# A graph layer on one NeuronCore: the maximum with zero of the messages moved from ScalarE to VectorE, and more rows fetched outside GpSimd

## The reference

```python
ef  = relu(edge_attr @ We1 + be1) @ We2 + be2        # 64 -> 128 -> 128
tw  = sigmoid(edge_weight[:, None] @ Wt + bt)
ef  = ef * tw
msg = relu(concatenate([x[src], ef], 1) @ Wn1 + bn1) @ Wn2 + bn2
out = segment_sum(msg, dst, num_segments=6250) + x
y   = layernorm(x + out)
```

## Time and profile before

| | |
|---|---|
| median of 3 runs | 1044.24 us (1042.26 to 1045.14) |
| the profiled execution | 1044.55 us |
| its span, first to last instruction | 1043.1 us |
| mean granted clock of TensorE | 0.956 of full speed |
| PE busy | 851.1 us (82%) |
| POOL busy | 776.5 us (74%) |
| DVE busy | 648.9 us (62%) |
| ACT busy | 494.9 us (47%) |

### The profile page before, as it was taken

One profiled execution on the slowest core, in us unless ns is written; L12 is line 12 of the kernel. 1 busy time (PEld: TensorE's weight loads), 2 busy tenths in 40 slices (PEclk: granted clock), 3 DMA queues, 4 the chain that ended last, 5 costly groups with the idle time before them and its releaser, 6 DMA issues.

```text
span 1043.1 us, 22424 instructions
## 1 busy us (share of the span) xinstructions
PE 851.1 (82%) x5035; PEld 616.5 (59%) x5036; DVE 648.9 (62%) x1682; ACT 494.9 (47%) x674; POOL 776.5 (74%) x825
## 2 busy tenths in 40 slices
PE   6989996988888778778787778878877877888884
PEld 6766665665556565555565555555555555565653
DVE  4767774775756665755557566566566566557566
ACT  5565454455445345444345445445444444444443
POOL 7777777777777777777777777777777777777772
PEclk9999999999999999999999999999999999999997
DMA  8984555555555554554545555455455455455311
GB/s 231 278 239 124 146 146 146 140 150 140 135 156 142 144 155 118 145 154 133 137 138 137 137 143 155 117 146 154 115 147 146 126 146 143 127 149 142 83 53 48
DMA packets 159417, 148.90 MB, mean 143 GB/s; under 512 B 123479, under 2 KB 127894, under 8 KB 159270
## 3 DMA queue, kind: packets, MB, share of 16 engines
q1 hardware_dynamic: 129062, 89.99, 31.0%
q0 software_dynamic: 26080, 53.46, 20.0%
q10 hardware_dynamic: 4128, 3.87, 1.2%
HBM read 140.85 MB, written 6.40 MB: 141 GB/s over the span
## 4 chain that ended last, share of the span: by engine, by line
POOL 44%; issue 22%; PE 12%; DMA 7%; DVE 6%; SPq 3%; ACT 3%; ACTq 1%; DVEq 1%; POOLq 0%
POOL gathered L566 44%; DMA gathered<-node_table,src_e 5%; PE psS L896 4%; PE psM L938 3%; PE psE L963 2%; DVE h L1220 2%; PE psH L951 2%; SPq L537 2%; DMA x_sb<-in_x 1%; DVE onehot L1226 1%; ACT h L656 1%; DMA ew<-in_edge_weight 1%; ACT tw L724 1%; ACTq L652 1%; DVE efw L1241 1%
## 5 line engine op out<-in xcount | busy, mean ns | idle before, releaser
L566 POOL DMA_INDIRECT gathered<-node_table,src_e x767 | 729.3, 951 | 234.0 <-issue 228.2
L729 ACT ACTIVATE h<-psH,be_c 128x1024 f32<-128x1024 f32 x104 | 115.9, 1114 | 443.1 <-PE psH L951 435.1
L896 PE MATMUL psS<-onehot,h 128*128 128x128 f32 x1656 | 226.4, 292 | 67.6 <-ACT h L656 65.7
L896 PEld LDWEIGHTS psS<-onehot,h 128*128 128x128 f32 x1656 | 209.1, 204 | 86.1 <-issue 49.4
L1220 DVE TENSOR_TENSOR h<-psM,gathered 128x1024 f32<-128x1024 f32 (+1 forms) x102 | 120.2, 1180 | 220.8 <-DMA gathered<-node_table,src_e 173.4
L963 PE MATMUL psE<-h,we 128*128 128x512 f32 x416 | 218.3, 649 | 0.0
L938 PE MATMUL psM<-wn,efw 128*128 128x128 f32 x1664 | 208.6, 280 | 4.8 <-DVE h L1220 4.8
L938 PEld LDWEIGHTS psM<-wn,efw 128*128 128x128 f32 x1664 | 200.7, 197 | 5.6 <-DVE h L1220 5.6
L1241 DVE SCALAR_TENSOR_TENSOR efw<-psE,be_c,tw 128x1024 f32<-128x1024 f32 x104 | 133.3, 1281 | 105.6 <-PE psE L963 95.5
L951 PE MATMUL psH<-eaT,we 64*128 64x512 f32 x416 | 120.1, 654 | 66.7 <-DMA gathered<-node_table,src_e 63.3
L1226 DVE TENSOR_SCALAR onehot<-split_ids,dst_e 128x65 f32<-128x65 f32 x832 | 173.9, 272 | 0.0
(11 more groups left out here) (128 smaller groups left out, 363.5 us busy)
## 6 DMA issues: line engine op xcount, KB each, us to landing
ew<-in_edge_weight SPq DMA_DIRECT2D x104, 512.0 KB
ea<-in_edge_attr SPq DMA_DIRECT2D x104, 256.0 KB
fetched<-node_table SPq DMA_DIRECT2D x1408, 0.5 KB
dst_rows<-node_table ACTq DMA_DIRECT2D x768, 0.5 KB
gathered<-node_table,src_e POOLq DMA_INDIRECT x767, 2.5
x_sb<-in_x SPq DMA_DIRECT2D x6, 512.0 KB, 9.0
out_y<-x_sb ACTq DMA_DIRECT2D x12, 256.0 KB
node_table<-gathered SPq DMA_DIRECT2D x7, 256.0 KB, 5.7
```

The lines of the kernel that those rows point to most:

```text
L566: pool.indirect_dma_start(to, None, rows, bass.IndirectOffsetOnAxis(index, 0)).then_inc(landed, by)
L729: nc.scalar.activation(h1[:, s % 2, :], psH[:, :, :].rearrange("p r e -> p (r e)"), ACT.Relu, bias=be1_c[:, :]).then_inc(h1_ready, 1)
L896: return nc.tensor.matmul(to, h[:, (k - SUM_LAG) % BODY * PAIR + q, t * C:(t + 1) * C], hot, start=(t == 0), stop=(t == TILES - 1))
```

## The change

- `FETCHED` starts a pair earlier and runs to pair 102: 12 pairs (14, 22, ..., 102) in place of 11. SP's loop gets two more rounds of `fetch_rows` at its end for it.
- `ACT_FETCHED` follows a list of parts: a first tile at 8 rows a step over 16 steps, then seven at 12 rows a step over 11 steps: 8 pairs (23, 33, 44, 55, 66, 77, 88, 99) in place of 6.
- `CLOSE_FROM` goes from 20 to 40.
- The relu of `h` goes from ACT. DVE makes the maximum with zero in place instead, by one `tensor_scalar` directly behind `pre`, after a wait for it. The last pair keeps its relu on ACT, and so does the first layer.
- In ACT's step the wait for `psS` stays where it was and the copy moves behind the block's copy.
- PE waits in `sums_step` for `sums_ready`, too: the relu that it waited for stood behind that copy on ACT.

```diff
-CLOSE_FROM = 20
+CLOSE_FROM = 40
...
-FETCHED = list(range(15, 96, FETCH_STEPS))
-ACT_ROWS, ACT_STEPS, ACT_FROM = 8, 16, 6
-ACT_FETCHED = list(range(ACT_FROM + ACT_STEPS, 103, ACT_STEPS))
+FETCHED = list(range(14, 103, FETCH_STEPS))
+ACT_FROM, ACT_PARTS = 6, [(8, 16)] + 7 * [(12, 11)]
+ACT_BEGIN = [ACT_FROM + sum(n for _, n in ACT_PARTS[:f]) for f in range(len(ACT_PARTS))]
+ACT_FETCHED = [at + n for at, (_, n) in zip(ACT_BEGIN, ACT_PARTS)]
+ACT_FETCHED = [p + (p in FETCHED) for p in ACT_FETCHED]
...
+            for n in range(PAIRS, FETCHED[-1] + 4):
+                fetch_rows(n)
...
-                f, at = divmod(s - ACT_FROM, ACT_STEPS)
-                if not 0 <= f < len(ACT_FETCHED) or at * ACT_ROWS >= P:
+                f = sum(s >= begin for begin in ACT_BEGIN) - 1
+                if f < 0:
+                    return
+                at, each = s - ACT_BEGIN[f], ACT_PARTS[f][0]
+                if at * each >= P:
                     return
...
                 if live(i, k, ADD_LAG):
-                    copy_sums(s - ADD_LAG, k - ADD_LAG)
+                    act.wait_ge(sum_ps, s - ADD_LAG + 1)
                 if TILE < k <= TILE + BT // 2 and 1 <= i < TURNS:
                     finish_one(act, blocks, low["now"], lambda b: copy_tiles((k - TILE - 1) * 2), False)
-                if live(i, k, H_LAG):
-                    g = s - H_LAG
-                    at = g % BODY * PAIR
-                    act.wait_ge(pre_ready, g + 1)
-                    relu(h[:, at:at + PAIR, :].rearrange("p q e -> p (q e)")).then_inc(h_ready, 1)
+                if live(i, k, ADD_LAG):
+                    copy_sums(s - ADD_LAG, k - ADD_LAG)
...
                     pe.wait_ge(h_ready, s - SUM_LAG + 1)
+                    if not (isinstance(i, int) and s == SUM_LAG):
+                        pe.wait_ge(sums_ready, s - SUM_LAG)
...
                 make_pre(h[:, at, :], psM[:, :, :], rows).then_inc(pre_ready, 1)
+                dve.wait_ge(pre_ready, g + 1)
+                to = h[:, at, :].rearrange("p q e -> p (q e)")
+                nc.vector.tensor_scalar(to, to, 0.0, None, ALU.max).then_inc(h_ready, 1)
```

More of the change, by code:

```diff
@@ L648, in fetch_rows @@
                     act.wait_ge(act_placed, f - 1)
-                parts = range(at * ACT_ROWS, min((at + 1) * ACT_ROWS, P))
+                parts = range(at * each, min((at + 1) * each, P))
                 rows = numbers_of(ACT_ENGINE, ACT_FETCHED[f], parts)
```

## The result

The changed kernel takes 1053.65 us (median of 5 runs, 1052.93 to 1058.01) against 1044.24 us: a ratio of 1.0108, 95% interval 1.0084 to 1.0132. It is slower, by 9.4 us, where 11.1 were forecast. The profiled execution took 1052.93 us, the shortest of the five, its span 1051.1 us.

The account below looks back on a forecast made before the run. GpSimd's stream of gathers was taken as the bound. 1044.55 - 3.8 (fewer gathers) + 14.2 (delayed gathers) + 0.7 (end) = 1055.65, less 0.3 for the median: 1055.3 us, range 1045 to 1062.

Parts of the forecast that it names:

- The bound: GpSimd's stream of 815 gathers, one each 1.256 us with no hole, sets the end; every other engine waits for it.
- Fetched rows: Row copies on SyncE and ScalarE for more pairs: three gathers go, -3.8 us; ScalarE's longer issues cost nothing.
- The third rival: ScalarE becomes the bound, its 12 issues slowing its step past GpSimd's 10 us: 1063 us and up; chance 0.02.
- The limit, ScalarE's order, TensorE's new wait: Running ahead limited from pair 40 for 20, sums copied later, TensorE waiting for copy and maximum: no effect on time.
- The maximum's time: Each of 103 maxima on VectorE, 128x1024 from SBUF to SBUF, takes 0.72 us, bounds 0.67 and 0.77.
- The delay of the gathers: Maxima on VectorE hold up gathers on GpSimd: 47 of 103 hit, 14.2 us in all.
- at one moment: A gather needs something of VectorE's only once, about 0.05 to 0.12 us after its start.
- The fourth rival: A gather has a second such moment, 0.74 to 0.94 us after its start: 1069 us; chance 0.04.
- the rule for the start: A gather's delay is the VectorE instruction's end minus the gather's start minus 0.12 us.
- The weighing of the Trainium skill's rule: VectorE and GpSimd's shared port: rows contradict VectorE being blocked when second; by the rule 11 us instead of 14.2.
- The end: The last maximum, of pair 102, ahead of VectorE's work on the last pair: 0.7 us, bounds 0 and 0.7.
- The first rival: The maximum holds up no gather, only the three fewer gathers count: 1040.5 us, 0.36% faster; chance 0.12.

Follow-up runs that it names:

- the kernels with short gathers and nothing late: Changed kernel with the relu back on ScalarE, 1040.12 us; changed kernel with the sum in PSUM and the maximum from PSUM to SBUF, 1041.20 us.
- the kernel at 1040.12 us: Changed kernel with the relu of the messages back on ScalarE, behind the copy of sums: 1040.12 us, ratio to before 0.9958.

## Why the prediction was right, and where it was not

**The bound** was read rightly: all differences sit in GpSimd's stream and behind it, and the kernels with short gathers and nothing late (1040.12 and 1041.20 us) differ from before by the number of gathers and by what lies behind the last one.

**Fetched rows**: -3.8 us forecast, -4.0 measured with the relu on ScalarE. Nothing for the longer list of issues was right at 12 rows, but the cover was thinner than I put it. Where 4.4 us of idle stood before the first layer, 28 steps now have the issues as the last thing before it, 132.0 us of such idle (3 steps and 8.0 us before); and 16 rows overran it. The third rival was misplaced by four rows a step, not in kind.

**The limit, ScalarE's order, TensorE's new wait**: nothing forecast and nothing found. The limit alone makes 1054.64 for 1053.65 us, within the spread; the order and the wait are in the kernel at 1040.12 us (the wait on TensorE names the copy there, and costs nothing that shows).

**The maximum's time**: 0.72 us forecast, 717 ns on average. It is 694 ns where it doesn't wait; the wait was not in the forecast.

**The delay of the gathers** is the term that was mis-sized: 14.2 us forecast, 11.0 measured. The cause was named rightly, the number of moments was not. Three errors lie in it, of both signs.
- At the gather's start I counted 47 hits; there were 42, worth 9.5 us, 4.7 less than forecast. I had let a maximum that begins up to 0.05 us after the gather's start hold it up for 0.6 us; such a maximum waits up to 0.03 us itself, and the gather goes free. With the adds of before that makes three hits too many, 1.9 us. Another 1.1 us is the length of 0.69 us for 0.72, and the rest is other phases. The two counts don't hold the same maxima: 16 of the 42 had waited at the second moment, and 14 of these would have ended too early for the next gather had they not.
- The second moment was missing. I took the tensor_scalar of 34.06 inside the gather of 33.79 as proof that one begun inside a gather costs nothing. It ended 0.74 us after the gather's start, before the 0.83 us from which an end costs anything; too short to show it. So the step "at one moment" of the prediction is wrong. The fourth rival had the second one, 0.74 to 0.94 us after the start, where no row reached and where the 0.83 us lies, and I gave it a chance of 0.04. It is there, but costs 5.6 us, not a second delay of the same size.
- What gathers take over 0.944 us each and no maximum accounts for was 6.0 us in all before and is 2.0 us after. That is a gain of 4.0 us that no step of the forecast has. Most of it are gathers that end late, by the rule for the start, behind an instruction with both inputs in SBUF: the node block's scalar_tensor_tensor and the adds to `acc`. They were 34 gathers and 4.5 us before, and are 13 and 1.7 us after; the rest lies in the set-up and in differences of a few ns. The number of these instructions is the same; their phases against the gathers are others. The kernels with the whole maximum from SBUF to SBUF have 0.4 to 1.7 us of it, and all others, the kernel before and the one with the maximum in PSUM (3.1 us) among them, 2.2 to 4.5, so it goes with the maximum. Why it does so isn't settled; that a VectorE which waits for a gather comes out of step with the next start would fit, and was not tested.

**The weighing of the Trainium skill's rule** has to be turned round in part. "SBUF — State Buffer", section "Who interferes with whom", says that whichever starts first has the shared pair and the other is blocked. I held that VectorE never waits. The maximum of 182.63 took 0.94 us for 0.69, so it does, as the page says; but not for the whole of a gather as the page has it, only in two short stretches of it, and a maximum that begins between them goes ahead (593.72). The estimate of 11 us by the page's rule meets the measured 11.0 by chance: it has 25 gathers delayed, and 81 were. The same page's section "SBUF: two separate sides" says that GpSimd cannot write descriptors while such an instruction runs; a gather held up late in its run fits that, though no row shows what it does then.

**The end**: 0.7 us forecast, 0.8 measured (16.95 us behind the last gather for 16.17; 16.4 with the relu on ScalarE).

**Sum**: -3.8 + 11.0 + 0.8 = +8.0 us of span, and the profiled run was the shortest of five; 1055.3 forecast, 1053.65 measured. The first rival fell with the first delayed gather. That the errors of the largest term (-4.7, +5.6 and -4.0 us) cancel to 3 us is luck: each of them is larger than that.

## What to carry to other kernels

Where a stream of indirect DMAs on GpSimd sets the time, a VectorE instruction with SBUF at both ends can have a price on that stream which its idle time doesn't show. Here the maximum had one, and so had the instructions with two inputs in SBUF; the one-hot tiles and the reductions had none. Look for gathers longer than the rest, and for what VectorE ran at their starts and late in their run. Reading from PSUM took the gathers' delay away here although the instruction became 0.5 us longer, and cutting the instruction in four took away two thirds: what counted is the length of one hold, not VectorE's work. And a queue that issues single rows has a step of its own: 12 rows were hidden here, 16 cost 30 us.

## What had not been expected of the hardware

- A gather of 128 rows and a maximum from SBUF to SBUF hold each other up at two moments of the gather's 0.94 us, about its start and late in its run (a maximum begun from 0.52 to 0.75 us waits until 0.77, one still running at 0.83 us delays the gather). Which of the two waits goes by their order: gathers took up to 1.46 us, maxima up to 0.94 us (694 ns alone).
- One-hot tiles and reductions, from SBUF to SBUF as well, held up no gather.
- Cost against length of one instruction, as time over the 1040.12 us without a maximum on VectorE: 454 ns, 1.6 us; 717 ns, 13.5 us; four of 312 ns, 4.0 us; 1225 ns from PSUM, 1.1 us, none of it in the gathers.
